# Graph attention on 8192 nodes: column groups for f, another order of loads and steps ahead of row 0, the mean in row 2, the last row on VectorE

## The chip, the cores and the metric

One core of a Trainium2 chip runs the kernel. The metric is device microseconds of one execution. TensorE is written PE (PEld is its weight load), VectorE DVE, ScalarE ACT, GpSimd POOL, SyncE SP; ACTq and SPq are the queues in which ACT and SP issue DMAs.

## The reference, cut to what matters

```python
h    = relu((x - mean(x)) / sqrt(var(x) + 1e-5))      # per row of x, 8192 x 256
g    = inlayer2 @ W.T + b                             # 8192 x 128
f1, f2 = g @ w1 + b1, g @ w2 + b2                     # one number per node each
L    = leaky_relu(f1[:, None] + f2[None, :], 0.01) - 1e9 * (adj == 0)
out  = x + softmax(L, axis=-1) @ h                    # adj is 8192 x 8192, int32
```

## The kernel before, in words

The output is made in 64 row tiles ("rows") of 128 nodes. For a row, the 128 x 8192 piece of adj (4 MB) comes in two halves (c = 0, 1) of four parts (g). ACT turns each part into a mask (L554), DVE makes unnormalised weights of it from the packed vectors `b_word` (per column) and `c_word` (per row) (`weights`, L824), DVE transposes them in eight strips of 1024 nodes (`turn`, L834) into one of four slots of `wT`, and PE multiplies each strip with the 16-bit parts of h in `H` (`products`, L1024 and L1026, 24 matmuls a strip), into `acc`. A 257th column gives the sum of weights. Then DVE makes its reciprocal (`finish_0` to `finish_2`, L843, L848, L853), ACT scales (`scale_rows`, L561), POOL adds x and, for a node with no neighbours, the mean of h (`finish`, L474, L476, L479), and SP stores. Each engine follows its own written list; semaphores order them.

Ahead of row 0 stands a start. inlayer2 (strips 0 to 7) and x (strips 0 to 7) are loaded in strips of 1024 nodes, 1 MB each, half issued by SP (quadrants 0, 1) and half by ACT (quadrants 2, 3). Since f1 and f2 are linear in inlayer2, `U` = W.T with w1 and w2 is made first; DVE transposes each strip of inlayer2 in two instructions (`turn_in2`, L718; there are two slots, so strip k waits for f of strip k - 2) and PE multiplies it with `V` (`f_of_strip`, L979): eight fp32 matmuls, one for each block of 32 features. `V` is made of the values of U spread over 128 columns, so that the results of the four quadrants of nodes stand apart. Strips 0 to 3 make chunk 0 of f, strips 4 to 7 chunk 1. ACT copies a chunk out of PSUM (`f_to_sbuf`, L532), DVE transposes it and takes the maximum (`chunk_f`, L751 to L756), PE and DVE bring the global maximum F to all partitions (L1003, L785, L1005), and from F come `D_big` and `D_inv` on ACT (L615, L616), the exponentials of b (`b_exponents` on PE, L987, then `b_of_chunk` on ACT, L537) and of c (L796, L1011, L622). DVE packs b and c (L809, L810), and `weights(0, 0, 0)` is the first of row 0 (L824 at 58.64 us).

The statistics of x are made beside that: strips 0 and 1 on ACT (`sums`, `squares`, L584), the others on DVE (`raw_stats`, L765, and `variance`, L773), the power of -1/2 on POOL (`rstds`, L411). Values of h are made by ACT and POOL and split into two 16-bit parts by ACT, POOL and DVE (`low_of_values`, L804). Rows 0 and 1 are interleaved by hand. The mean of h is summed by PE in between (`sum_of_values`, L1038), scaled by DVE (`h_sum`, L918), spread by PE (`hm_ps`, L1071) and copied by DVE (`h_mean`, L954); POOL's `finish` of row 0 waits for it, and SP, whose list has the store of row 0 ahead of the load of row 4's adj, waits for that `finish`.

Of the kernel before, what the change touches and what calls it, by code (L numbers as in the profile page):

```python
# [27 lines left out]
ALU = mybir.AluOpType  # L28
# [7 lines left out]
P = 128  # L36
B = 32
# [8 lines left out]
def graph_attention(nc, x, adj, inlayer2, W, b, w1, b1, w2, b2, out):  # L46
# [26 lines left out]
    with ExitStack() as ctx:  # L73
# [65 lines left out]
        F_ps = small[:, 1, 384:385]  # L139
        hs_ps = small[:, 1, 0:D]  # L140
# [37 lines left out]
        def h_slot(n):  # L178
# [4 lines left out]
        V = h_f32[:, 1, :, :].rearrange("p t d -> p (t d)").rearrange(  # L183
            "p (m i) -> p m i", m=FM)
# [25 lines left out]
        f_rows_ready = sem("f_rows_ready")  # L210
        f2_of_ready = sem("f2_of_ready")
# [46 lines left out]
        o_ready = sem("o_ready")  # L258
        o_stored = [sem(f"o_stored{i}") for i in range(2)]
# [103 lines left out]
        def _(sp):  # L363
# [4 lines left out]
            load_x(sp, 1, 4, (0, 1))  # L368
# [17 lines left out]
            for i in range(2):  # L386
                sp.wait_ge(o_ready, ROWS - 1 + i)
                sp.dma_start(out_rows[ROWS - 2 + i], o_sb[:, i, :]).then_inc(o_stored[i], 16)
            for i in range(2):
                sp.wait_ge(o_stored[i], 16 * ROWS // 2)  # L390

        @block.gpsimd
        def _(pool):
# [6 lines left out]
            rstd_order = (0, 2, 1, 3, 4, 5, 6, 7)  # L400
# [69 lines left out]
            def finish(I, par, half):  # L470
                pool.wait_ge(o_stored[par], 16 * half)
# [52 lines left out]
        def _(act):  # L524
# [94 lines left out]
            b_of_chunk(1)  # L619
            values(0)  # L620
# [67 lines left out]
            for i in range(2):  # L688
                scale_rows(ROWS - 2 + i, i, ROWS // 2 - 1)

        @block.vector
        def _(dve):
# [83 lines left out]
            for k in range(2, NS):  # L776
                turn_in2(k)
# [326 lines left out]
```

## Time and profile before

| | |
|---|---|
| runs of before | 1448.3, 1448.55, 1449.22 us; median 1448.55 |
| profiled execution | 1447.21 us; its span 1445.4 us |
| PE busy | 1408.1 us (97%) |
| DVE busy | 1279.7 us (89%) |
| granted clock, mean | 0.989 of 2.4 GHz |

The span runs from the first to the last instruction or landing of the program; 1.81 us of the profiled time lie around it. Busy shares are averages: the start, the passage into row 2 and the end have limits of their own. An engine's `xN` counts records; each fp32 matmul makes two.

### The profile page before, as it was taken

How to read it: one execution, taken by the hardware profiler on the slowest of the kernel's cores; microseconds unless marked ns; L12 is line 12 of the kernel's file. 1: busy time of each engine (PE TensorE's matmuls, PEld its weight loads, DVE VectorE, ACT ScalarE, POOL GpSimd, SP SyncE). 2: the span in 40 equal slices, each digit the busy share in tenths (PEclk: the TensorE clock that was granted, in tenths of full speed). 3: DMA queues.
4: the chain of work that ended last, by engine and by line, in shares of the span. 5: the costliest groups of instructions: out<-in, count | busy, mean ns of one | idle time of the engine just before them, and what ended most of it. 6: DMA issues, size and time to landing. Idle time of an engine off the chain costs nothing.

```text
span 1445.4 us, 33386 instructions
## 1 busy us (share of the span) xinstructions
PE 1408.1 (97%) x12623; PEld 1246.3 (86%) x12623; DVE 1279.7 (89%) x1313; ACT 612.4 (42%) x714; POOL 267.6 (19%) x269
## 2 busy tenths in 40 slices
PE   8489999999999999999999999999999999999998
PEld 7377888888888888888888888888888888888887
DVE  5899999989899898989989898998989989898994
ACT  2895344344444343444434344343434434344430
POOL 0582111101111110111111011111101111110111
PEclk9789999999999999999999999999999999999999
DMA  9978999999999999999999999999999999999940
GB/s 301 310 181 181 234 230 230 231 232 220 208 211 215 209 211 209 215 209 210 215 209 210 207 216 211 209 215 209 210 207 217 209 211 215 207 212 207 215 103 8
DMA packets 110168, 302.43 MB, mean 209 GB/s; under 512 B 11716, under 2 KB 44612, under 8 KB 110148
## 3 DMA queue, kind: packets, MB, share of 16 engines
q1 hardware_dynamic: 100144, 289.58, 89.4%
q10 hardware_dynamic: 10004, 12.59, 2.9%
q8 instruction: 12, 0.20, 0.1%
q14 instruction: 8, 0.07, 0.0%
HBM read 293.73 MB, written 8.39 MB: 209 GB/s over the span
## 4 chain that ended last, share of the span: by engine, by line
PE 94%; ACT 2%; DVE 2%; DMA 1%; issue 1%; ACTq 0%; POOL 0%; SPq 0%; POOLq 0%; DVEq 0%
PE acc L1024 61%; PE acc L1026 30%; PE rp L979 2%; DMA adj_sb<-in_adj_dram 1%; DVE wgt L824 1%; ACT h_f L570 1%; DVE wT L834 0%; ACT H L576 0%; PE rp L993 0%; ACT o_room L584 0%; DMA w<-in_L_gnn_w_dram 0%; PE small L966 0%; ACT rp L554 0%; DVE b_word L810 0%; ACT mask L554 0%
## 5 line engine op out<-in xcount | busy, mean ns | idle before, releaser
L1024 PE MATMUL acc<-H,wT 128*128 128x257 f16 x8192 | 1356.2, 273 | 9.7 <-DVE wT L834 6.9
L1026 PE MATMUL acc<-H,wT 128*128 128x257 f16 x4096 | 1120.0, 273 | 0.0
L1024 PEld LDWEIGHTS acc<-H,wT 128*128 128x128 bf16 x8192 | 802.1, 98 | 113.0 <-DVE wT L834 6.9
L554 ACT ACTIVATE mask<-adj_sb 128x1024 bf16<-128x1024 int32 x504 | 519.2, 1053 | 542.8 <-DVE wgt L824 428.8
L834 DVE STREAM_TRANSPOSE wT<-wgt 128x1024 f32<-128x1024 f32 x512 | 634.0, 1239 | 129.2 <-PE acc L1026 129.1
L824 DVE SCALAR_TENSOR_TENSOR wgt<-b_word,c_word,mask 128x1024 f32<-128x1024 f32 x504 | 626.9, 1256 | 0.0
L1026 PEld LDWEIGHTS acc<-H,wT 128*128 128x128 f16 x4096 | 401.5, 98 | 50.5
L474 POOL TENSOR_TENSOR x_res<-o_room,x_res 128x256 f32<-128x256 f32 x64 | 66.5, 1039 | 1115.2 <-ACT o_room L561 1069.5
L561 ACT ACTIVATE o_room<-acc,r_den 128x256 f32<-128x256 f32 x64 | 30.2, 471 | 251.0 <-DVE r_den L853 251.0
L479 POOL TENSOR_TENSOR o_room<-o_room,x_res 128x256 f32<-128x256 f32 x64 | 82.3, 1287 | 5.3
L476 POOL TENSOR_SCALAR o_room<-h_mean,no_nb 128x256 f32<-128x256 f32 x64 | 60.8, 950 | 0.0
L979 PE MATMUL rp<-wT,h_f 128*128 128x256 f32 x128 | 28.0, 381 | 0.0
L979 PEld LDWEIGHTS rp<-wT,h_f 128*128 128x128 f32 x128 | 24.5, 192 | 3.3
L570 ACT ACTIVATE h_f<-H,h_add,h_mul 128x256 f32<-128x256 f32 x48 | 24.7, 588 | 1.0 <-issue 1.0
L467 POOL TENSOR_TENSOR H<-h_f,H 128x1024 f16<-128x1024 f32 x8 | 17.8, 2226 | 4.0 <-ACT H L576 4.0
L411 POOL TENSOR_TENSOR rstd<-var_eps,minus_half 128x8 f32<-128x8 f32 x8 | 14.7, 1845 | 13.8 <-DVE var_eps L773 13.7
L1045 PE MATMUL small<-ones 128*128 128x128 f32 x20 | 4.6, 429 | 11.8 <-DVE wgt L824 11.8
L765 DVE BATCH_NORM_STATS2 stats<-H 128x6 f32<-128x512 f32 x24 | 15.3, 688 | 0.8 <-DMA H<-in_x_dram 0.8
L843 DVE TENSOR_SCALAR no_nb<-acc 128x1 f32<-128x1 f32 x64 | 7.7, 120 | 9.2 <-PE acc L1026 9.2
L1045 PEld LDWEIGHTS small<-ones 128*128 128x128 f32 x20 | 4.3, 331 | 12.0 <-DVE wgt L824 12.0
L718 DVE STREAM_TRANSPOSE wT<-wgt 128x1024 f32<-128x1024 f32 x8 | 9.5, 1222 | 5.7 <-DMA wgt<-in_L_gnn_inlayer_dram 3.6
L718 DVE STREAM_TRANSPOSE wT<-adj_sb 128x1024 f32<-128x1024 f32 x8 | 9.5, 1225 | 4.3 <-PE rp L979 4.3
(91 smaller groups left out, 173.2 us busy)
## 6 DMA issues: line engine op xcount, KB each, us to landing
adj_sb<-in_adj_dram SPq DMA_DIRECT2D x504, 512.0 KB, 8.6
x_res<-in_x_dram SPq DMA_DIRECT2D x64, 128.0 KB, 4.0
out_dram<-o_room SPq DMA_DIRECT2D x64, 128.0 KB, 4.2
H<-in_x_dram ACTq DMA_DIRECT2D x16, 256.0 KB, 12.2
H<-in_x_dram SPq DMA_DIRECT2D x16, 256.0 KB, 12.7
adj_sb<-in_adj_dram ACTq DMA_DIRECT2D x8, 512.0 KB, 13.1
wgt<-in_L_gnn_inlayer_dram ACTq DMA_DIRECT2D x8, 256.0 KB, 9.0
wgt<-in_L_gnn_inlayer_dram SPq DMA_DIRECT2D x8, 256.0 KB, 9.6
```

The source lines that it names most:

```text
L474: nc.gpsimd.tensor_tensor(x_res[:, par, :], o_raw[:, par, :], x_res[:, par, :], ALU.add).then_inc(pool_step, 1)
L476: nc.gpsimd.tensor_scalar(o_sb[:, par, :], h_mean[:, :], no_nb[:, par:par + 1], None, ALU.mult).then_inc(pool_step, 1)
L479: nc.gpsimd.tensor_tensor(o_sb[:, par, :], o_sb[:, par, :], x_res[:, par, :], ALU.add).then_inc(o_ready, 1)
L554: nc.scalar.activation(place, adj_sb[:, c, g * CQ:(g + 1) * CQ], ACT.Relu, scale=M_SCALE).then_inc(m_ready, 1)
L561: nc.scalar.activation(o_raw[:, par, :], acc[:, par, 0:D], ACT.Copy, scale=r_den[:, par:par + 1]).then_inc(scaled, 1)
L570: nc.scalar.activation(h_slot(n)[:, t, :], x_stage(n // 2)[:, j % TS, :], ACT.Relu, scale=h_mul[:, j:j + 1], bias=h_add[:, j:j + 1]).then_ ...
L718: nc.vector.transpose(in2T[:, k % 2, :, :].rearrange("p m (t s) -> p t m s", t=TS)[:, HALF * e:HALF * (e + 1), :, :], in2_stage(k)[:, HALF ...
L824: nc.vector.scalar_tensor_tensor(out=wgt[:, wgt_slot(I, c), g, :], in0=b_word[:, c * CQ:(c + 1) * CQ], scalar=c_word[:, bass.ds(Q * I + g, ...
L834: nc.vector.transpose(wT[:, wT_slot(I, k), :, :].rearrange("p t (g r) -> p g t r", g=Q), wgt[:, wgt_slot(I, c), :, s * SQ:(s + 1) * SQ]).t ...
L979: mm = pe.matmul(rp[:, k // SC, SQ * (k % SC):SQ * (k % SC + 1)], V[:, m, :], in2T[:, k % 2, m, :], start=(m == 0), stop=(m == FM - 1))
L1024: pe.matmul(acc[:, par, 0:DV], w_hi[:, slot, t, :], H[:, j, part, 0:DV], start=(j == 0 and part == 0), stop=False)
L1026: mm = pe.matmul(acc[:, par, 0:DV], w_lo[:, slot, t, :], H[:, j, 0, 0:DV], start=False, stop=(j == ROWS - 1))
```

## The change

1. Start, f: `V` has 32 columns instead of 128. Each strip's eight matmuls are 128 x 32 x 256, the four blocks of an inner loop going to four groups of 32 output partitions, in two rounds. The four groups hold partial sums; after DVE's transpose of a chunk, PE adds them with four small matmuls (`f_sums`), and DVE takes the sum from there. Behind each strip PE gets four fp32 matmuls of ones into a scratch place (`keep_busy(4)`).
2. Start, order: x strip 1 is loaded ahead of inlayer2 strips 6 and 7; ACT's part of strip 7 of inlayer2 is issued behind `sums(0)`. On DVE the transpose and maximum of chunk 0 stand ahead of strip 7, the statistics of x strips 2 and 3 in other places. On ACT `squares(1)` stands ahead of `f_to_sbuf(1)`, and ACT's two issues for x strip 7 stand behind `b_of_chunk(1)`. On POOL `rstds(1)` comes earlier and `rstds(3)` later.
3. Row 2: `h_sum`, its matmul and `h_mean` leave the passage between rows 1 and 2. DVE makes `h_sum` in strip step 0 of row 2, PE spreads it behind strip 1, DVE copies `h_mean` in step 5 instead of 2.
4. End: the last row is finished by two instructions on DVE, and its store is issued in two halves, by SP and by ACT.

```diff
-            load_in2(eng, 4, 8, quadrants)
+            load_in2(eng, 4, 6, quadrants)
+            load_x(eng, 1, 2, quadrants)
...
+            load_in2(sp, 6, 8, (0, 1))
-            load_x(sp, 1, 4, (0, 1))
+            load_x(sp, 2, 4, (0, 1))
...
-                for m in range(FM):
-                    mm = pe.matmul(rp[:, k // SC, SQ * (k % SC):SQ * (k % SC + 1)], V[:, m, :], in2T[:, k % 2, m, :],
-                                   start=(m == 0), stop=(m == FM - 1))
+                for e in range(2):
+                    for g in range(Q):
+                        m = 2 * g + e
+                        mm = pe.matmul(rp[B * g:B * (g + 1), k // SC, SQ * (k % SC):SQ * (k % SC + 1)], V[:, m, :],
+                                       in2T[:, k % 2, m, :], start=(e == 0), stop=(e == 1))
                 mm.then_inc(f_done, 1)
+            def f_sums(c):
+
+                pe.wait_ge(f_cols_ready, c + 1)
+                pe.wait_ge(pick_ready, Q + 1)
+                parts = f_cols[:, c * CQ:(c + 1) * CQ].rearrange("p (j a o v) -> p a j o v", a=Q, o=2, v=Q)
+                for a in range(Q):
+                    mm = pe.matmul(f_sum_ps[B * a:B * (a + 1), c * ROWS:(c + 1) * ROWS], same[:, :],
+                                   parts[:, a, :, :, 0], start=True, stop=True)
+                mm.then_inc(f_sum_ps_ready, 1)
...
+            def keep_busy(n):
+                for _ in range(n):
+                    pe.matmul(acc[:, 0, 0:P], ones[:, :], ones[:, :], start=True, stop=True)
...
-            dve.wait_ge(h_sum_done, 1)
-            nc.vector.tensor_scalar(h_sum[:, :], hs_ps, 1.0 / (H_SCALE * N), None, ALU.mult).then_inc(h_sum_ready, 1)
             weights(2, 2, 0)
...
-                    if is_row(I, 2) and u == 2:
+                    if is_row(I, 2) and u == 0:
+                        dve.wait_ge(h_sum_done, 1)
+                        nc.vector.tensor_scalar(h_sum[:, :], hs_ps, 1.0 / (H_SCALE * N), None,
+                                                ALU.mult).then_inc(h_sum_ready, 1)
+                    if is_row(I, 2) and u == 5:
...
+            nc.vector.scalar_tensor_tensor(out=x_res[:, 1, :], in0=acc[:, 1, 0:D], scalar=r_den[:, 1:2],
+                                           in1=x_res[:, 1, :], op0=ALU.mult, op1=ALU.add).then_inc(last_sum, 1)
+            dve.wait_ge(last_sum, 1)
+            nc.vector.scalar_tensor_tensor(out=o_sb[:, 1, :], in0=h_mean[:, :], scalar=no_nb[:, 1:2],
+                                           in1=x_res[:, 1, :], op0=ALU.mult, op1=ALU.add).then_inc(last_ready, 1)
```

PE, from the last warm-up ahead of f to the one ahead of row 0, in the kernel before (`rp<-wT,h_f` is f of a strip, `rp<-mask` the exponents of b, `tiny` the maximum):

```order
L993 MATMUL rp<-ones 128x128 x9
L979 MATMUL rp<-wT,h_f 128x256 x64
L987 MATMUL rp<-mask 128x512 x2
L1003 MATMUL small<-ident,tiny 1x128
L1005 MATMUL small<-tiny,ones 128x1
L987 MATMUL rp<-mask 128x512 x2
L1011 MATMUL small<-low,mask 128x64 x4
L1045 MATMUL small<-ones 128x128 x10
```

PE in the changed kernel, from strip 5 on (`acc<-ones` is the filler, `small<-wgt,same` is `f_sums`):

```order
L1020 MATMUL rp<-wT,h_f 32x256 x8
L1012 MATMUL acc<-ones 128x128 x4
L1020 MATMUL rp<-wT,h_f 32x256 x8
L1012 MATMUL acc<-ones 128x128 x4
L1030 MATMUL small<-wgt,same 32x64 x4
L1020 MATMUL rp<-wT,h_f 32x256 x8
L1012 MATMUL acc<-ones 128x128 x4
L1038 MATMUL rp<-mask 128x512 x2
L1030 MATMUL small<-wgt,same 32x64 x4
L1069 MATMUL small<-ident,tiny 1x128
L1071 MATMUL small<-tiny,ones 128x1
L1038 MATMUL rp<-mask 128x512 x2
```

Between the last transposed strip and F stand now the fillers, two sums over the groups, and the first exponents of b ahead of the second sum.

DVE in the kernel before, from the transposes of inlayer2 strips 4 to 7 on (two instructions a strip; `BN_STATS` is `raw_stats`):

```order
L718 STREAM_TRANSPOSE wT<-adj_sb 128x4x8x32 x8
L751 STREAM_TRANSPOSE wgt<-mask 128x1024
L752 COPY f_col<-wgt 128x64
L754 TENSOR_REDUCE tiny<-f_col 128x1
L765 BN_STATS stats<-H 128x6 x2
L751 STREAM_TRANSPOSE wgt<-mask 128x1024
L752 COPY f_col<-wgt 128x64
L754 TENSOR_REDUCE tiny<-f_col 128x1
L756 TENSOR_TENSOR tiny<-tiny 128x1
L765 BN_STATS stats<-H 128x6 x2
L783 TENSOR_TENSOR tiny<-cst 128x1
L785 TENSOR_REDUCE tiny<-small 1x1
```

DVE in the changed kernel, from the same strips on:

```order
L731 STREAM_TRANSPOSE wT<-adj_sb 128x4x8x32 x6
L764 STREAM_TRANSPOSE wgt<-mask 128x1024
L770 COPY f_col<-small 128x64
L772 TENSOR_REDUCE tiny<-f_col 128x1
L731 STREAM_TRANSPOSE wT<-adj_sb 128x4x8x32 x2
L783 BN_STATS stats<-H 128x6 x4
L764 STREAM_TRANSPOSE wgt<-mask 128x1024
L770 COPY f_col<-small 128x64
L772 TENSOR_REDUCE tiny<-f_col 128x1
L774 TENSOR_TENSOR tiny<-tiny 128x1
L791 TENSOR_SCALAR var_eps<-stats 128x8
L808 TENSOR_TENSOR tiny<-cst 128x1
```

Strip 7 now stands behind the transpose of chunk 0 and behind a copy that needs PE's sum over the groups, and the second chunk behind all statistics of x strip 2.

DVE at the passage into row 2, from the reciprocal of row 0 on, in the kernel before:

```order
L853 RECIPROCAL r_den<-den 128x1
L918 TENSOR_SCALAR h_sum<-small 128x256
L824 SCALAR_TENSOR_TENSOR wgt<-b_word,c_word,mask 128x1024 x2
L834 STREAM_TRANSPOSE wT<-wgt 128x4x8x32
L824 SCALAR_TENSOR_TENSOR wgt<-b_word,c_word,mask 128x1024 x2
L834 STREAM_TRANSPOSE wT<-wgt 128x4x8x32
L824 SCALAR_TENSOR_TENSOR wgt<-b_word,c_word,mask 128x1024
L834 STREAM_TRANSPOSE wT<-wgt 128x4x8x32
L954 COPY h_mean<-small 128x256
```

and in the changed kernel:

```order
L875 RECIPROCAL r_den<-den 128x1
L846 SCALAR_TENSOR_TENSOR wgt<-b_word,c_word,mask 128x1024 x2
L856 STREAM_TRANSPOSE wT<-wgt 128x4x8x32
L846 SCALAR_TENSOR_TENSOR wgt<-b_word,c_word,mask 128x1024
L976 TENSOR_SCALAR h_sum<-small 128x256
L846 SCALAR_TENSOR_TENSOR wgt<-b_word,c_word,mask 128x1024
L856 STREAM_TRANSPOSE wT<-wgt 128x4x8x32
L846 SCALAR_TENSOR_TENSOR wgt<-b_word,c_word,mask 128x1024
L856 STREAM_TRANSPOSE wT<-wgt 128x4x8x32
```

`h_sum` has gone behind the first weights that follow row 2's first transpose, and the copy of `h_mean` out of this stretch.

## Rows read from the trace of the kernel before

**Rows 1.** The page, part 1 (busy time) and part 2 (granted clock in 40 slices)
```profile
PE 1408.1 (97%) x12623; PEld 1246.3 (86%) x12623; DVE 1279.7 (89%) x1313; ACT 612.4 (42%) x714; POOL 267.6 (19%) x269
...
PEclk9789999999999999999999999999999999999999
```

**Rows 2.** Windows: busy time (records) of each engine, granted clock, DMA share, GB/s
```profile
58.73:110.06 51.33, 38.58 (x357) 31.53 (x357) 51.23 (x52) 49.22 (x73) 43.74 (x57) 0.79 0.84 206
...
132.58:1439.55 1306.97, 1306.97 (x11880) 1162.29 (x11880) 1168.62 (x1171) 524.31 (x546) 206.19 (x189) 1.00 0.93 206
```

**Rows 3.** Waits of PE, 0 to 150 us: total us, times, longest
```profile
PE acc L1024 <- DVE wT L834: 6.9, 5, 4.3
```

**Rows 4.** Timeline, start: start us, length us, engine, line, instruction [idle before]
```profile
14.52 28.01 PE L979 MATMUL rp<-wT,h_f 128*128 128x256 f32 x128
...
35.73 2.37 DVE L718 STREAM_TRANSPOSE wT<-adj_sb 128x1024 f32<-128x1024 f32 x2 [1.08 <-PE rp L979]
...
37.34 0.42 ACT L584 ACTIVATE o_room<-H 128x256 f32<-128x256 f32 x1 [3.41 <-DMA H<-in_x_dram]
...
38.03 1.20 DVE L751 STREAM_TRANSPOSE wgt<-mask 128x1024 f32<-128x1024 f32 x1
```

**Rows 5.** The last two inlayer2 issues of each queue: durations, starts, time to landing
```profile
L333 ACTq DMA_DIRECT2D adj_sb<-in_L_gnn_inlayer_dram x2: 1397/1964/2532, 18.6 to 21.2; - x2
...
DMA to landing us min/median/max: 11.9/12.8/13.2
```

**Rows 6.** Timeline of ACT and its queue behind the last strip of f
```profile
42.57 1.01 ACT L532 COPY mask<-rp 128x1024 f32<-128x1024 f32 x1 [1.68 <-PE rp L979]
...
46.46 2.85 ACTq L333 DMA_DIRECT2D H<-in_x_dram  x1
...
49.34 1.42 ACTq L333 DMA_DIRECT2D H<-in_x_dram  x1
...
50.80 0.26 ACT L615 ACTIVATE D_big<-f_rel 128x64 f32<-128x64 f32 x1 [3.27 <-issue]
```

**Rows 7.** Windows (columns as in rows 2), then timeline: VectorE up to the first weights
```profile
35.73:58.64 22.91, 12.18 (x51) 8.42 (x49) 18.21 (x35) 16.32 (x47) 8.80 (x10) 0.87 1.08 333
...
58.64 1.27 DVE L824 SCALAR_TENSOR_TENSOR wgt<-b_word,c_word,rp 128x1024 f32<-128x1024 f32 x1
```

**Rows 8.** Timeline of PE: ten warm-up matmuls; then windows of PE alone
```profile
63.57 4.64 PE L1045 MATMUL small<-ones 128*128 128x128 f32 x20 [11.83 <-DVE wgt L824]
...
86.60:90.05 3.45, 0.00 (x0) 1.00 0.95 255
90.05:93.50 3.45, 2.86 (x14) 0.51 1.02 274
```

**Rows 9.** Timeline, passage from row 1 to row 2, PE and VectorE
```profile
124.91 0.42 DVE L918 TENSOR_SCALAR h_sum<-small 128x256 f32<-128x256 f32 x1 [2.30 <-PE small L1038]
...
127.44 0.60 PE L1071 MATMUL small<-h_sum,ones 128*128 128x256 f32 x2
129.15 0.38 PE L1024 MATMUL acc<-H,wT 128*128 128x257 f16 x2 [1.11 <-DVE wT L834]
...
132.58 0.39 PE L1024 MATMUL acc<-H,wT 128*128 128x257 f16 x2 [0.63 <-DVE wT L834]
```

**Rows 10.** Timeline, the mean vector, SyncE's load of row 4, its mask
```profile
134.76 0.39 DVE L954 COPY h_mean<-small 128x256 f32<-128x256 f32 x1
...
139.90 5.07 SPq L338 DMA_DIRECT2D adj_sb<-in_adj_dram  x8
...
152.94 2.00 ACT L554 ACTIVATE mask<-adj_sb 128x1024 bf16<-128x1024 int32 x2 [9.58 <-DMA adj_sb<-in_adj_dram]
```

**Rows 11.** Timeline, the end, VectorE, ScalarE, SyncE's queue
```profile
1439.97 0.16 DVE L853 RECIPROCAL r_den<-den 128x1 f32<-128x1 f32 x1
1440.17 0.47 ACT L561 ACTIVATE o_room<-acc,r_den 128x256 f32<-128x256 f32 x1 [17.00 <-DVE r_den L853]
...
1443.23 0.34 SPq L388 DMA_DIRECT2D out_dram<-o_room  x1
```

More of the change, by code:

```diff
@@ L139, in graph_attention @@
         F_ps = small[:, 1, 384:385]
+        f_sum_ps = small[:, 0, 256:256 + 2 * ROWS]
         hs_ps = small[:, 1, 0:D]
@@ L258, in graph_attention @@
         o_ready = sem("o_ready")
+        last_sum = sem("last_sum")
+        last_ready = sem("last_ready")
+        last_stored = sem("last_stored")
         o_stored = [sem(f"o_stored{i}") for i in range(2)]
@@ L687, in _ @@
             row_tiles(act, body, ahead=1)
-            for i in range(2):
-                scale_rows(ROWS - 2 + i, i, ROWS // 2 - 1)
+            scale_rows(ROWS - 2, 0, ROWS // 2 - 1)
+            act.wait_ge(last_ready, 1)
+            act.dma_start(out_rows[ROWS - 1][P // 2:P], o_sb[P // 2:P, 1, :]).then_inc(last_stored, 16)
         @block.vector
@@ L774, in variance @@
                                         ALU.add).then_inc(var_ready, 1)
-            for k in range(2, NS):
-                turn_in2(k)
-            chunk_f(0)
+            turn_in2(2)
+            turn_in2(3)
+            turn_in2(4)
+            turn_in2(5)
+            turn_in2(6)
+            chunk_turn(0)
+            chunk_max(0)
+            turn_in2(7)
             raw_stats(16, 20)
-            chunk_f(1)
             raw_stats(20, 24)
+            chunk_turn(1)
+            chunk_max(1)
+            variance(2)
             dve.wait_ge(u_ready, Q + 1)
@@ L856, in _ @@
             then_wait(pack_b(0))
+            raw_stats(28, 32)
             then_wait(pack_b(1))
+            variance(3)
             dve.wait_ge(c_exp, 1)
@@ L994, in _ @@
             pe.wait_ge(u_ready, Q)
-            for k in range(NS):
-                f_of_strip(k)
+            f_of_strip(0)
+            keep_busy(4)
+            f_of_strip(1)
+            keep_busy(4)
+            f_of_strip(2)
+            keep_busy(4)
+            f_of_strip(3)
+            keep_busy(4)
+            f_of_strip(4)
+            keep_busy(4)
+            f_of_strip(5)
+            keep_busy(4)
+            f_of_strip(6)
+            keep_busy(4)
+            f_sums(0)
+            f_of_strip(7)
+            keep_busy(4)
             pe.wait_ge(f2_of_ready, 1)
             b_exponents(0)
+            f_sums(1)
             pe.wait_ge(ident_ready, 1)
@@ L1069, in _ @@
             products(1, 1, 7)
-            pe.wait_ge(h_sum_ready, 1)
-            pe.matmul(hm_ps, ones[:, :], h_sum[:, :], start=True, stop=True).then_inc(h_mean_ps_ready, 1)
             pe.wait_ge(scaled, 1)
@@ L1080, in body @@
                     products(I, par, k)
+                    if is_row(I, 2) and k == 1:
+                        pe.wait_ge(h_sum_ready, 1)
+                        pe.matmul(hm_ps, ones[:, :], h_sum[:, :], start=True,
+                                  stop=True).then_inc(h_mean_ps_ready, 1)
             row_tiles(pe, body, ahead=1)
```

64 lines of the change are left out of this document (37 added, 27 removed).

## The prediction

> **What bounds the kernel now.** I read the page first. PE is busy for 97% of the span and its clock is at the full level in nearly all slices [rows 1]: almost all of the time is matmuls that this change leaves alone. So the next question is where PE last waited, and the windows answer it: from 132.58 to 1439.55 us PE has no idle time [rows 2]. That stretch holds 495 strips, 2.640 us each. Nothing that happens on another engine there costs anything, as long as it stays inside its cover. The time can change in three places only: in what ends at 132.58, in the 5.85 us behind 1439.55, and by a new stall in between.
>
> Then I ask what sets 132.58. The waits of PE show 6.9 us on DVE's transposes up to 150 us [rows 3], 4.3 of them in one piece. DVE is busy for 51.23 of 51.33 us between 58.73 and 110.06 [rows 2]. So in rows 0 and 1 DVE is the bound, and PE's stalls there are its echo. DVE gets through this list as early as it may begin it: its beginning is the first `weights`, at 58.64 [rows 7]. A microsecond at 58.64 is, to first order, one at the end. Ahead of 58.64, DVE is busy for only 18.21 of 22.91 us [rows 7]; the 4.70 idle us are what the start can still give. The last 110 to 133 us have a limit of their own, the passage into row 2.
>
> **Sum, term 1: the start (f).** Before, the 128 records of f take 28 us without a pause, 3.48 us a strip [rows 4], which is slower than a strip's two transposes (2.37): DVE waits 1.08 us each time for PE. In column groups, a strip's 16 records would take a quarter if the four run side by side, 0.87 us; no row here shows such groups, so my bounds are that quarter and all of the 3.48. That removes the PE bound, but not what is below it: the last issues of inlayer2 start at 21.2 us and need up to 13.2 to land [rows 5], so the last strip is there at 34.3, and before it was transposed at 35.73. No more than 1.4 us could be had there. And now x strip 1 takes that place in the queues: strip 6 lands at 34.3, strip 7 where x strip 1 landed. ACT waited for x strip 1 until 37.34 [rows 4], so strip 7 is there 3 us later than now. The work on DVE from strip 6 on is then the 18.21 us of before and one more strip: 34.3 + 2.37 + 18.21 = 54.9 us, and to that come the waits. This is the place where the order of the change matters. Strip 7 is put behind `chunk_max(0)`, which needs PE: f of strip 6, four fillers, `f_sums(0)`.
>
> With PE at full clock: strip 6 transposed at 36.7; f 0.87, fillers 8 records of 128 columns, 0.87 (half of a 256-column record's 0.217 each), sums about 0.5 with latency: 39.0 to 39.2. DVE has the transpose of chunk 0 (1.20 [rows 4]) meanwhile, until 37.9; it waits 1.3. For chunk 1 PE has f, fillers and the first exponents of b (about 3.6 together) against DVE's statistics and transpose (3.8): a wait of about 0.6. The two steps to F cost 0.7, small gaps 0.5 as before (4.70 less the three long waits). First `weights`: 54.9 + 1.3 + 0.6 + 0.7 + 0.5 = 58.0, or 0.6 us earlier than now. ACT's move of x strip 7 belongs to this term: in the trace the two issues block the ScalarE list for 2.85 and 1.42 us and D_big stands at 50.80 [rows 6]; without them b is ready up to 2 us earlier, but DVE, full by then with moved statistics, uses little of that.
>
> **The clock decides the term.** PE now has 1.7 us of work a strip, fillers included. An issue takes some 1.4 us in the full queue [rows 5], two a strip in each queue, so strips come every 2.8 us. Strip 5 is two places ahead of strip 6, with x strip 1 between: landed by 28.7, transposed by 31.1, done on PE at 32.8. Then PE has nothing until 36.7, about 4 us. What PE did before its clock fell in this trace: no record from 86.60 to 90.05, and then a window at 0.51 although PE was 83% busy in it [rows 8]. The gap ahead of strip 6 is about as long as the wait around that one, 4.3 us [rows 3]. At the low level ten fp32 matmuls of 128 columns take 4.64 us, 0.213 us a record once running [rows 8], twice as long. Then f of strip 6 takes 1.74, fillers 1.71 and sums 0.6: 41.0 instead of 39.1, 1.8 us lost. The fillers, meant as cover, lie on the path here. If the clock is back by the end of this burst (4 us without a pause; between 90.05 and 93.50 it came back after such a one), chunk 1 runs at full rate: first `weights` at 59.8, **1.2 us later than now**. I take this value. If it is low in chunk 1 too, f, fillers and exponents take 7 us against DVE's 3.8: another 3.5 to 4 us, first `weights` at about 63.7, 5 us later.
>
> The Trainium skill, page "TensorE: Matmul & The Clock Gate", Part 1 (HAM oscillation), says that short bursts of matmuls with waits for DMA between them start cold each time; the window at 0.51 agrees with it. The same page, Part 3, gives 2.38 times for three column tiles side by side; by that figure f would take 1.46 us a strip, an estimate, and the first `weights` would stand about a microsecond later. No row of this trace can bear that figure out.
>
> **Term 2: into row 2.** DVE waits 2.30 us for PE's sum and needs 0.42 for `h_sum` [rows 9]; without them the weights and the first transpose of row 2 come 2.65 us earlier, at 126.3. PE is then free at 127.44, instead of starting strip 0 at 129.15 [rows 9]. Strip 0 ends at 130.08. Strip 1's transpose ended at 132.55 and ends at 132.55 - 2.65 + 0.42 = 130.3 (0.42 for `h_sum`, now in its path): 0.2 stall. Strip 1 ends at 132.94, the matmul for the mean takes 0.43, strip 2 starts at 133.4; before it was 132.58 + 2.64 = 135.22. Gain 1.8 us.
>
> What is late next: `h_mean`. It moves from 134.76 to behind strip 5, in my count 139.8. POOL's `finish` waits for it, SP's store waits for POOL, and behind the store in SP's list are row 4's loads, issued at 139.90 [rows 10], when the reads had nothing else to do. They go out at about 145.0, and the first masks move from 152.94 to 158.0, done at 159.0. DVE wants them at about 156.3 (from 139.8 on: the copy, eight weights, eight transposes at 1168.62 / 990 = 1.18 each plus gaps). It waits 2.7 us, does two weights and a transpose until 162.7; PE wants that strip at 133.4 + 11 x 2.64 = 162.4. So 0.3 us come back. Net 1.5.
>
> **Term 3: the end.** The reciprocal ends at 1440.13, the store is issued at 1443.23 [rows 11]; between them an ACT and three POOL instructions. Two DVE instructions of 128x256 take their place. The kernel before has none of that kind; `h_sum`, one input from PSUM, took 0.42 [rows 9], a 1024-column weights 1.27 (a quarter is 0.32) [rows 7], ACT's scaling 0.47 [rows 11]. I take 0.42 each: store issued at 1441.1. The two halves land about as the whole did, 2.2 us later. Gain 2.15, bounds 1.9 to 2.4.
>
> **Sum.** -1.2 + 1.5 + 2.15 = 2.45 us less. Against the profiled execution's own 1447.21 this is 1444.8; the median of the runs stands 1.34 above it, so 1448.55 - 2.45 = **1446.1**.
>
> **Rivals.**
> - *The clock stays up (or is back within strip 6).* For: fillers behind each strip, and strips 4 and 5 follow closely. Against: the gap of 4 us. First `weights` 58.0: 0.6 + 1.5 + 2.15 = 4.25, 1444.3.
> - *The start gets clearly shorter.* f ends early, DVE finds its data, the 4.70 us of idle shrink to 2: 1442.5. Against: strip 7 lands 3 us later than before.
> - *Low clock through chunk 1.* For: DVE-paced bursts of 1.7 us. -5 + 1.5 + 2.15: slower by 1.4, 1449.9, too little to be told from no change.
> - *Column groups don't run side by side, at low clock.* Each strip then needs 6.9 us: strip 6's f, fillers and sums end at 46, DVE waits 8 us instead of 1.3, and strip 7's f (3.5 at full rate) adds 2.6. First `weights` at 67.4: -8.8 + 1.5 + 2.15, slower by 5.1, 1453.7. The side changes where the start loses more than 3.65 us, and is measurable beyond 6.5. For: in the trace every fp32 record takes its full time, whatever it feeds. Against: the four groups use different columns of the array.
> - *Row 4's loads too late.* Each further microsecond on POOL or in the loads is one of PE stall in row 3, at strip 5; 1 to 2 us, 1447.5. POOL's first `finish` has such spread.
>
> **How the numbers follow.** I give 0.40 to the forecast (own range 1445.0 to 1447.5, a quarter of it beyond the bound of "faster"), 0.27 to the clock staying up, 0.06 to the shorter start, 0.14 to the low clock through chunk 1, 0.07 to groups in series, 0.06 to row 4. About 0.2% (2.9 us) is what a measurement of this kernel can tell from no change: faster means below 1445.65. Faster: 0.27 + 0.06 + 0.10 = 0.43. Slower: 0.07 and a part of the low clock's spread, 0.11. The rest, 0.46, is the same. The range is 1443.3 to 1450.0: it leaves out the shortest start and the series.
>
> **What the profile after would show.** Term 1: the granted clock between 30 and 50 us; f of a strip in 0.9 us (1.7 if low) or in 3.5; DVE waiting for PE between the two chunks; the first `weights` at 59.8. Term 2: row 2 starting with no wait over 0.3 us, no stall of PE at about 162. Term 3: two instructions of 0.4 us and a span that ends 3.7 us behind the last matmul instead of 5.85. I am wrong if the first `weights` move and the end doesn't follow, which would mean that DVE's list from 58.73 to 110.06 has slack, in its waits for POOL inside instructions for example.

## The result, and the profile after

Over 16 runs the changed kernel takes 1452.68 us (1448.59 to 1454.83), the kernel before 1448.70 us (1447.25 to 1449.38) on the same chips. The ratio is 1.0025, with a 95% interval of 1.0018 to 1.0032: slower by 0.25%, about 4 us. The profiled execution of after took 1454.47 us (span 1452.7), 7.3 us more than the profiled one of before.

Part 1 and part 2 of the page of after, the rows that answer to [rows 1], and then the longest waits of PE in its first 190 us (total, times, longest):

```profile
PE 1405.4 (97%) x12703; PEld 1236.8 (85%) x12703; DVE 1281.2 (88%) x1315; ACT 611.2 (42%) x713; POOL 265.7 (18%) x266
...
PEclk9789999999999999999999999999999999999999
...
PE rp L1020 <- DVE wT L731: 11.2, 5, 5.0
PE acc L1090 <- DVE wT L856: 4.9, 2, 4.5
PE acc L1090 <- ACT o_room L572: 3.6, 1, 3.6
```

Against [rows 1] PE is busy 2.7 us less, in a span 7.3 us longer. In the waits there are two new ones, on the transposes of inlayer2 (L731) in the start and on `o_room`, which ScalarE writes (L572). The old wait on `wT`, 6.9 us in [rows 3], is now 4.9 us in two pieces.

**Start.** Timeline of PE in after, from f of strip 4 on (start, length, engine, line, instruction, idle before and what ended it):

```profile
28.95 1.94 PE L1020 MATMUL rp<-wT,h_f 128*32 128x256 f32 x16 [5.00 <-DVE wT L731]
30.82 2.08 PE L1012 MATMUL acc<-ones 128*128 128x128 f32 x8
...
38.04 1.94 PE L1020 MATMUL rp<-wT,h_f 128*32 128x256 f32 x16 [2.33 <-DVE wT L731]
39.91 1.76 PE L1012 MATMUL acc<-ones 128*128 128x128 f32 x8
41.60 0.41 PE L1030 MATMUL small<-wgt,same 128*32 128x64 f32 x8
44.98 1.94 PE L1020 MATMUL rp<-wT,h_f 128*32 128x256 f32 x16 [2.97 <-DVE wT L731]
46.84 1.70 PE L1012 MATMUL acc<-ones 128*128 128x128 f32 x8
```

A strip of f takes 1.07 us at full clock and 1.94 at half; before it took 3.48 [rows 4]. The clock was down for strip 4 already (5.00 us idle ahead of it), and for strips 6 and 7 and the fillers behind them. In between it came back: the granted clock was 0.50 from 38 to 41 us, 1.00 from 42 to 44 us, where PE waited for strip 7, and 0.50 again from 45 to 48 us. Its mean from 14.46 to 45.00 us was 0.83. VectorE in the same stretch and up to the first `weights`:

```profile
35.62 2.37 DVE L731 STREAM_TRANSPOSE wT<-adj_sb 128x1024 f32<-128x1024 f32 x2 [3.69 <-DMA adj_sb<-in_L_gnn_inlayer_dram]
...
42.07 0.22 DVE L770 COPY f_col<-small 128x64 f32<-128x64 f32 x1 [2.96 <-PE small L1030]
...
42.55 2.37 DVE L731 STREAM_TRANSPOSE wT<-adj_sb 128x1024 f32<-128x1024 f32 x2
...
62.42 1.26 DVE L846 SCALAR_TENSOR_TENSOR wgt<-b_word,c_word,rp 128x1024 f32<-128x1024 f32 x1
```

Strip 6 is transposed at 35.62, with 3.69 us of idle time ahead of it for its load, and strip 7 only at 42.55, because `chunk_max(0)` (L770) stands ahead of it and waits 2.96 us for PE. The first `weights` stand at 62.42 instead of 58.64 [rows 7]: 3.8 us later.

**Row 2 and row 3.** Timeline of VectorE, PE, POOL, SyncE's queue and ScalarE around the mean vector and the masks of row 4, and a window (busy time and records of each engine, granted clock, DMA share, GB/s):

```profile
136.37 0.60 PE L1147 MATMUL small<-h_sum,ones 128*128 128x256 f32 x2
...
143.06 0.38 DVE L980 COPY h_mean<-small 128x256 f32<-128x256 f32 x1
...
143.52 1.70 POOL L485 TENSOR_TENSOR x_res<-o_room,x_res 128x256 f32<-128x256 f32 x1 [25.82 <-DVE h_mean L980]
...
147.57 0.36 SPq L389 DMA_DIRECT2D out_dram<-o_room  x1
...
148.82 4.68 SPq L343 DMA_DIRECT2D adj_sb<-in_adj_dram  x8
...
161.50 3.90 ACT L565 ACTIVATE mask<-adj_sb 128x1024 bf16<-128x1024 int32 x4 [14.33 <-DMA adj_sb<-in_adj_dram]
171.18 3.90 ACT L565 ACTIVATE mask<-adj_sb 128x1024 bf16<-128x1024 int32 x4 [5.78 <-DMA adj_sb<-in_adj_dram]
174.98 0.45 ACT L572 ACTIVATE o_room<-acc,r_den 128x256 f32<-128x256 f32 x1
...
166.46 0.40 PE L1090 MATMUL acc<-H,wT 128*128 128x257 f16 x2 [0.46 <-DVE wT L856]
...
175.56 0.61 PE L1090 MATMUL acc<-H,wT 128*128 128x257 f16 x2 [3.65 <-ACT o_room L572]
...
170.00:182.00 12.00, 8.35 (x52) 6.14 (x50) 10.95 (x9) 4.98 (x6) 3.32 (x3) 0.72 1.03 224
```

The passage itself went as forecast: PE has no wait there, and the matmul of the mean takes 0.60 us. But the copy of `h_mean` is at 143.06 instead of 134.76, and row 4's loads at 148.82 instead of 139.90 [rows 10]. The second half of the masks starts at 171.18, and ScalarE's scaling stands behind it, at 174.98; in the kernel before it was at 165.62, behind masks that began at 161.81:

```profile
161.81 3.90 ACT L554 ACTIVATE mask<-adj_sb 128x1024 bf16<-128x1024 int32 x4 [4.97 <-DMA adj_sb<-in_adj_dram]
165.62 0.46 ACT L561 ACTIVATE o_room<-acc,r_den 128x256 f32<-128x256 f32 x1
```

PE has to have that scaling ahead of strip 7 of row 3, and idles for 3.65 us. From 170 to 182 us its granted clock is 0.72: this wait is followed by a stretch at half clock, in which a pair of matmuls takes up to 0.64 us instead of 0.38, until 181.2 us.

**End.** The last instructions of VectorE and the two halves of the last store:

```profile
1448.90 0.48 DVE L989 SCALAR_TENSOR_TENSOR x_res<-acc,r_den,x_res 128x256 f32<-128x256 f32 x1
1449.41 0.48 DVE L992 SCALAR_TENSOR_TENSOR o_room<-h_mean,no_nb,x_res 128x256 f32<-128x256 f32 x1
...
1449.93 0.55 SPq L396 DMA_DIRECT2D out_dram<-o_room  x1
...
1449.93 0.57 ACTq L702 DMA_DIRECT2D out_dram<-o_room  x1
```

They answer to [rows 11]: the stores are issued 1.07 us behind the end of the reciprocal (1448.86) instead of 3.10, but the span ends 2.77 us behind the issue instead of 2.2.

The start's 3.8 us are 3.5 by the last transposes of row 1 (112.29 against 108.75). So the profiled executions differ by 3.5 (start) - 1.9 (passage) - 1.4 (end) and what is left for row 3, 7.1, together 7.3 us. The 7.1 is a remainder; the first experiment checks it.

### The profile page after: what moved, and what is told of

The parts are those of the page before. It is cut to its first block, busy times and chain, and to the rows that moved or that the text cites. A ratio compares the mean times of both kernels' runs of the same rounds, so it can differ in the third digit from the quotient of the medians.

```text
span 1452.7 us, 33546 instructions
## 1 busy us (share of the span) xinstructions
PE 1405.4 (97%) x12703; PEld 1236.8 (85%) x12703; DVE 1281.2 (88%) x1315; ACT 611.2 (42%) x713; POOL 265.7 (18%) x266
## 4 chain that ended last, share of the span: by engine, by line
PE 88%; ACT 3%; DMA 3%; SPq 2%; DVE 2%; issue 1%; POOL 0%; ACTq 0%; DVEq 0%; POOLq 0%
PE acc L1090 58%; PE acc L1092 29%; DMA adj_sb<-in_adj_dram 2%; ACT mask L565 1%; SPq L338 1%; ACT h_f L581 1%; DMA adj_sb<-in_L_gnn_inlayer_dram 1%; ACT H L587 0%; ACT rp L565 0%; SPq L343 0%; PE rp L1020 0%; DVE stats L783 0%; DVE wgt L846 0%; PE acc L1012 0%; DVE b_word L832 0%
## 5 line engine op out<-in xcount | busy, mean ns | idle before, releaser
L856 DVE STREAM_TRANSPOSE wT<-wgt 128x1024 f32<-128x1024 f32 x512 | 633.7, 1239 | 131.2 <-PE acc L1092 131.1
L572 ACT ACTIVATE o_room<-acc,r_den 128x256 f32<-128x256 f32 x63 | 29.8, 473 | 228.8 <-DVE r_den L875 228.8
L1020 PE MATMUL rp<-wT,h_f 128*32 128x256 f32 x128 | 11.9, 506 | 11.2 <-DVE wT L731 11.2
L731 DVE STREAM_TRANSPOSE wT<-adj_sb 128x1024 f32<-128x1024 f32 x8 | 9.5, 1224 | 9.2 <-DMA adj_sb<-in_L_gnn_inlayer_dram 9.1
L1020 PEld LDWEIGHTS rp<-wT,h_f 128*32 128x32 f32 x128 | 4.1, 134 | 15.2 <-DVE wT L731 12.2
L1012 PEld LDWEIGHTS acc<-ones 128*128 128x128 f32 x64 | 9.7, 233 | 4.8 <-issue 4.8
```

The source lines that it names most:

```text
L572: nc.scalar.activation(o_raw[:, par, :], acc[:, par, 0:D], ACT.Copy, scale=r_den[:, par:par + 1]).then_inc(scaled, 1)
L856: nc.vector.transpose(wT[:, wT_slot(I, k), :, :].rearrange("p t (g r) -> p g t r", g=Q), wgt[:, wgt_slot(I, c), :, s * SQ:(s + 1) * SQ]).t ...
L1020: mm = pe.matmul(rp[B * g:B * (g + 1), k // SC, SQ * (k % SC):SQ * (k % SC + 1)], V[:, m, :], in2T[:, k % 2, m, :], start=(e == 0), stop=( ...
```

## Experiments

All times are medians in us, beside the kernel before on the same chip (1448.57 to 1448.96). Each kernel was run 10 or 11 times, the ninth, twelfth and fifteenth 5 times. The theory: in row 2 nothing is wrong but the place of `h_mean`, whose delay reaches PE a row later; and the start is late by itself. The rivals stand in each expectation.

**1. The copy of h_mean behind strip 3.** The kernel after with

```diff
-                    if is_row(I, 2) and u == 5:
+                    if is_row(I, 2) and u == 3:
```

Expected: 

> The kernel after, with the copy of h_mean on VectorE two places earlier (behind strip 3 of row 2 instead of strip 5). Theory A: the loss comes in row 3, where PE waited 3.65 us at strip 7 for ScalarE's scaling (behind late masks) and its clock then fell for 7 us. With the copy 4 to 5 us earlier, that stall and the fall of the clock are gone: 3.8 us less (what is left of the medians' difference of 4.0 after +3.5 for the start, -1.9 for the passage, -1.4 for the end) to 7.1 us less (what the profiled execution shows): 1445.6 to 1448.9, likeliest 1447. Theory B: the loss is the late start, and the wait at strip 7 is the luck of one execution: 1452 to 1453, as after.

Measured: 1447.15 (1445.1 to 1449.29, 11 runs), ratio to before 0.9985 [0.9976, 0.9994]. One digit takes 5.5 us off and turns slower into faster. Its window over the same 12 us, and the issue and the scaling that moved:

```profile
143.01 5.68 SPq L343 DMA_DIRECT2D adj_sb<-in_adj_dram  x8
...
165.83 3.90 ACT L565 ACTIVATE mask<-adj_sb 128x1024 bf16<-128x1024 int32 x4 [6.56 <-DMA adj_sb<-in_adj_dram]
169.64 0.45 ACT L572 ACTIVATE o_room<-acc,r_den 128x256 f32<-128x256 f32 x1
...
170.00:182.00 12.00, 12.00 (x112) 10.68 (x110) 11.74 (x14) 3.99 (x5) 3.48 (x3) 1.00 1.03 229
```

PE runs 112 records in these 12 us, 0.107 us each; after had 52, so 60 x 0.107 = 6.4 us were lost there, 3.65 of them idle and some 2.8 by the clock (an upper bound, since some records can be missing).

**2 and 3. The row 2 part alone, on the kernel before**, once with `h_mean` behind strip 5 and once behind strip 3:

```diff
-            dve.wait_ge(h_sum_done, 1)
-            nc.vector.tensor_scalar(h_sum[:, :], hs_ps, ...)
...
+                    if is_row(I, 2) and u == 0:
+                        dve.wait_ge(h_sum_done, 1)
...
-                    if is_row(I, 2) and u == 2:
+                    if is_row(I, 2) and u == 5:    # 3 in the other
```

Expected with 5: 

> The kernel before with the row 2 part of the change alone (h_sum and its matmul inside row 2, h_mean behind strip 5). Theory A: 1.9 us earlier into row 2, h_mean 4.7 us later, so that the loads of row 4 go out 4.7 us later; ScalarE's scaling then ends 3.2 us behind the time at which PE wants it at strip 7 of row 3, and the fall of the clock costs up to 3.4 more: 1450.0 to 1453.4. Theory B (the loss is in the start; this part is worth what was predicted): 1.5 us faster than before, 1447.2.

Expected with 3: 

> As the second kernel, but h_mean copied behind strip 3. Theory A: the passage's 1.9 us come, and the loads of row 4 go out at about 140, as before; no stall at strip 7 of row 3: 1446.8. Theory B: the same as with strip 5, within 0.5 us. A third theory, that the matmul of the mean inside row 2 is itself the cost, gives 1449 or more here too.

Measured: 1452.70 (ratio 1.0023 [1.0014, 1.0032]) and 1446.94 (0.9986 [0.9977, 0.9995]). In the first PE waits for ScalarE at the same place:

```profile
173.12 0.45 ACT L561 ACTIVATE o_room<-acc,r_den 128x256 f32<-128x256 f32 x1
...
173.71 0.61 PE L1026 MATMUL acc<-H,wT 128*128 128x257 f16 x2 [4.48 <-ACT o_room L561]
```

A loss as large as that of the whole change appears with this part alone, and the same part with the copy two strips earlier is worth 2.0 us, what the prediction had for the passage (1.8).

**4. The end alone, on the kernel before** (the diff's parts on `finish`, the last two stores and the two VectorE instructions). Expected: 

> The kernel before with the end part alone: the last row finished by two VectorE instructions, its store in two halves. From the profile after, 4.4 us behind the last matmul instead of 5.85: 1.4 us less, 1447.3. The prediction had 2.15 less, 1446.5. A rival, that the two stores end no sooner than one: 1448.7.

Measured: 1447.31, 1.65 us less (0.9988 [0.9979, 0.9997]).

**5. SyncE's list reordered, h_mean still behind strip 5.** In SyncE's list the store of row 0 and the load of row 2's x (`x_res`) go from ahead of row 4's loads to between their two halves; for that the list of one more pair of rows is written out (`ahead=2`). The kernel after with

```diff
+                    if is_row(I, 3) and n == Q - 1:
+                        sp.wait_ge(o_ready, 1)
+                        sp.dma_start(out_rows[0], o_sb[:, 0, :])...
+                        sp.dma_start(x_res[:, 0, :], x_rows[2])...
-                    if n == NS - 1 and not (is_row(I, 0) or is_row(I, 1)):
+                    if n == NS - 1 and not (is_row(I, 0) or is_row(I, 1) or is_row(I, 2)):
...
-            row_tiles(sp, body, ahead=1)
+            row_tiles(sp, body, ahead=2)
```

Expected: 

> The kernel after with h_mean left behind strip 5, but in SP's list row 0's store and the residual load of row 2 stand behind the first mask loads of row 4 instead of ahead of them. Theory A (what makes the late h_mean costly is the order of SP's list: its store waits for h_mean by way of POOL, and row 4's loads stand behind it): the loads go out at about 140 to 143 us, no stall at strip 7 of row 3, and the time is that of the run with the earlier copy, 1447.2, within 0.7. Theory B (the late copy costs by another way, on VectorE or POOL): as after, 1452 to 1453.

Measured: 1447.12 (0.9989 [0.9980, 0.9998]), as the first experiment. SyncE's queue in it:

```profile
134.50 1.74 SPq L343 DMA_DIRECT2D adj_sb<-in_adj_dram  x4
...
147.82 0.36 SPq L389 DMA_DIRECT2D out_dram<-o_room  x1
...
148.70 1.88 SPq L343 DMA_DIRECT2D adj_sb<-in_adj_dram  x4
```

The copy is as late as in after (143.31), and so is row 0's store at 147.82. But the four loads of the first half are out at 134.50, ahead of it (I had expected 140). They land from 146.1 to 152.9, and the other four, issued at 148.70, from 156.3 to 163.5; the last one of after lands at 171.09. PE does not wait. What costs is the order of SyncE's list, by way of ScalarE's, and not the late copy as such.

**6, 7 and 9. The fillers of the start**, all with the copy behind strip 3. Sixth: 22 matmuls behind strip 3, 12 behind strip 5, 9 ahead of strip 7, the others as they were. Seventh: no fillers. Ninth: none on the path from strip 6 on, and long ones in the waits behind strips 3, 5 and 6; those behind strips 0, 1, 2 and 4 stay:

```diff
             f_of_strip(3)
-            keep_busy(4)
+            keep_busy(22)
...
             f_of_strip(5)
-            keep_busy(4)
+            keep_busy(20)
             f_of_strip(6)
-            keep_busy(4)
             f_sums(0)
+            keep_busy(12)
             f_of_strip(7)
-            keep_busy(4)
```

Expected of the sixth: 

> As the first experiment (copy behind strip 3), and the fillers of TensorE made long enough to cover its waits for the strips of inlayer2: 22 matmuls instead of 4 behind strip 3, 12 behind strip 5, 9 ahead of strip 7. Theory C (the start is late because the clock is down when strips 6 and 7 come): the clock stays up from 15 to 55 us, f of strips 6 and 7 and the fillers behind them take 2 us each time instead of 3.7, the first weights stand at 59 to 60 instead of 62.4, and the time falls by 2 to 3 us to 1444.2 to 1445.2. Theory D (the landing of strip 7 and the work on VectorE behind it set the start, whatever the clock): within 0.7 of 1447.15.

Expected of the seventh: 

> As the first experiment, with all the 4-matmul fillers between the strips of f taken out. Theory C2 (in this execution the fillers did not hold the clock, and stood on the path behind strips 6 and 7 with 1.7 us each): the clock falls earlier, but f_sums(0) and the exponents of b come up to 1.7 us earlier each; first weights 1.5 to 3 us earlier, 1444.5 to 1446. The rival, that the fillers were worth their time: at the lower clock the chain behind them costs more than they did, 1448 or more.

Expected of the ninth: 

> As the first experiment (copy behind strip 3), but fillers only where TensorE has nothing else to do: 22 matmuls behind strip 3, 20 behind strip 5, none behind strip 6, 12 behind f_sums(0), none behind strip 7. In the run with 22, 12 and 9 (first weights 60.27, median 1445.3) the clock had fallen again for f of strip 6, and it and its fillers took 3.8 us ahead of f_sums(0). If clock and fillers on the path are what is left, VectorE gets f_sums(0) and f_sums(1) 2.2 to 2.5 us earlier, of which ScalarE's values of b let it use two thirds: first weights 58.3 to 58.9, time 1443.4 to 1444. If the landing of strip 7 sets the start, it stays at 1445.0 to 1445.6.

Measured: 1445.30, 1445.43 and 1442.72, against 1447.15. The seventh fell into its range; the sixth just missed its range (1444.2 to 1445.2), and the ninth gave 0.7 us more than its own (1443.4 to 1444). No fillers at all is better than the fillers of the change, although the clock is then at 0.50 from 30 to 40 us. In the sixth f of strip 6 still took 1.94 us, behind 2.08 us of idle time:

```profile
37.20 1.94 PE L1020 MATMUL rp<-wT,h_f 128*32 128x256 f32 x16 [2.08 <-DVE wT L731]
39.06 1.89 PE L1012 MATMUL acc<-ones 128*128 128x128 f32 x8
```

In the ninth the idle time ahead of it is 0.33 us, f takes 1.07, and `f_sums(0)` follows at once:

```profile
37.59 1.07 PE L1020 MATMUL rp<-wT,h_f 128*32 128x256 f32 x16 [0.33 <-DVE wT L731]
38.72 0.41 PE L1030 MATMUL small<-wgt,same 128*32 128x64 f32 x8
39.05 2.94 PE L1012 MATMUL acc<-ones 128*128 128x128 f32 x24
```

The first `weights` stood at 60.27, 60.82 and 57.90, the last 0.4 us ahead of what I had given it.

**8 and 12. The kernel before with row 2 (behind strip 3) and the end, without and with the x issue moved:**

```diff
-            load_x(act, 7, 8, (2, 3))
             act.wait_ge(f2_rel_ready, 1)
...
             b_of_chunk(1)
+            load_x(act, 7, 8, (2, 3))
```

Expected without: 

> The kernel before with the row 2 part (h_mean behind strip 3) and the end part, and its own start. If the two add: 1448.96 - 2.02 - 1.65 = 1445.3. The difference to the first experiment is then what the start part costs: 1.9 us by the medians, against 3.5 to 3.8 by the first weights of one profiled execution. If they do not add (a stall moved to the next row): 1446.5 or more.

Expected with: 

> The kernel before with row 2 (h_mean behind strip 3), the end part and the last x issue moved behind the values of b on ScalarE, its start otherwise its own. The run without the move took 1445.17. If the issue delays D_big and with it b on the path (VectorE waited 1.6 to 2.7 us for b ahead of the first weights in the runs with before's start), the move gives 1 to 2 us: 1443.2 to 1444.2. If x strip 7 lands too late for its first reader, or VectorE was not waiting for ScalarE's list, no change: 1445.2.

Measured: 1445.17, as expected, and 1442.49 (0.9959 [0.9945, 0.9972]), 0.7 us below the range that I had given. The move alone is worth 2.7 us. ScalarE's exponential of f (`D_big`), in the eighth and then in the twelfth, shows why:

```profile
46.21 4.40 ACTq L336 DMA_DIRECT2D H<-in_x_dram  x1
50.64 1.50 ACTq L336 DMA_DIRECT2D H<-in_x_dram  x1
52.18 0.26 ACT L622 ACTIVATE D_big<-f_rel 128x64 f32<-128x64 f32 x1 [5.07 <-issue]
```

```profile
48.48 0.26 ACT L621 ACTIVATE D_big<-f_rel 128x64 f32<-128x64 f32 x1 [1.23 <-DVE f_rel L798]
```

**10 and 11. The loads in their old order.** Tenth: inlayer2 strips 4 to 7 ahead of x strip 1 again. Eleventh: besides, strip 7 transposed straight behind strip 6, `f_sums(0)` behind the first exponents, no fillers behind strips 6 and 7, and 22 instead of 4 behind strip 3.

Expected of the tenth: 

> As the first experiment, with the first loads in the order of before: inlayer2 strips 4 to 7, then x strip 1 and on, column groups, fillers and VectorE's order as in the kernel after. If the change of the load order is what makes the start late (VectorE sat idle 3.7 us ahead of strip 6, waiting for its load), strip 6 lands some 2.3 us earlier, and the first weights come that much earlier than 62.5: median 1444.9 to 1445.2. If x strip 1 is then missed just as much by ScalarE and by VectorE's statistics, no gain: 1446.8 to 1447.5.

Expected of the eleventh: 

> As the run with the loads in the order of before, and besides strip 7 transposed straight behind strip 6 instead of behind chunk_max(0), f of strips 6 and 7 back to back without fillers, f_sums(0) behind the first exponents of b, and 22 fillers behind strip 3. It has column groups, but not the other edits of the start. Strips 6 and 7 land at 32.5 and 34.3, transposed by 37.2 (35.73 + 2.37 = 38.1 in the kernel before): the limit by loads that the prediction gave, 0.9 us ahead of before, at most 1.4. First weights 58 to 59, 3.5 to 4.5 us earlier than the first experiment's 62.5: 1442.7 to 1443.7. If the extra step through PE (f_sums) costs as much as the groups save: 1445.2, as with before's own start.

Measured: 1446.43 and 1446.69; both missed, by 1.2 and 3 us, and both lie outside the rivals' values too. In the eleventh strips 6 and 7 were transposed by 37.9, close to the 37.2 that I had given them. Timeline of ScalarE and VectorE in the eleventh:

```profile
46.62 0.99 ACT L541 COPY mask<-rp 128x1024 f32<-128x1024 f32 x1
...
44.02 0.23 DVE L767 COPY f_col<-small 128x64 f32<-128x64 f32 x1 [5.01 <-PE small L1027]
```

Now x strip 1 is the late one. ScalarE's list has its sums and squares ahead of the copy of f's second half out of PSUM (L541), and this one comes at 46.62 (46.65 in the tenth), 6.7 us behind the matmuls that it copies; and VectorE waits 5.01 us for `f_sums(0)`, which stands on PE behind the exponents of b at the half clock (3.78 us).

**13. The x issue moved, alone, on the kernel before.** Expected: 

> The kernel before with the last x issue moved, and nothing else. With the row 2 and end parts beside it the move gave 2.7 us (1445.17 to 1442.49). If the parts add: 1448.85 - 2.7 = 1446.1. If the move only pays once row 2 is mended: 1447.5 or more. The prediction had counted it at next to nothing.

Measured: 1446.25 (0.9983 [0.9974, 0.9992]), 2.3 us less.

**14. The first experiment with the x issue back in its old place.** Expected: 

> As the first experiment (the kernel after, copy behind strip 3), with the last x issue back in its old place, ahead of the wait for F in ScalarE's list. If the move pays in the changed start too, this is 2.7 us slower than 1447.15: 1449.9, and the column groups, fillers and load order together then cost 4.7 us by themselves. If in the changed start the move pays nothing, because ScalarE is idle there before F comes (D_big at 53 instead of 51): 1447.2, and what the change of the start gives away is that the move is no longer worth its 2.7.

Measured: 1447.39 (0.9991 [0.9982, 1.0000]); the rival was right, no difference to 1447.15. The same instruction there:

```profile
46.91 4.90 ACTq L338 DMA_DIRECT2D H<-in_x_dram  x6
53.11 0.26 ACT L627 ACTIVATE D_big<-f_rel 128x64 f32<-128x64 f32 x1 [5.19 <-DVE f_rel L813]
```

**15. The eleventh, mended.** ScalarE's list is that of the kernel before but for the last x issue: the copies of f's rows stand ahead of the squares, and x strip 4 is issued ahead of the sums of strip 1. `f_sums(0)` stands straight behind f of strip 7, and 7 fillers between strips 6 and 7. The part on f's second half:

```diff
-            squares(1)
             f_to_sbuf(1)
             load_x(act, 5, 6, (2, 3))
+            squares(1)
...
             f_of_strip(6)
+            keep_busy(7)
             f_of_strip(7)
+            f_sums(0)
             pe.wait_ge(f2_of_ready, 1)
             b_exponents(0)
-            f_sums(0)
```

Expected: 

> As the run with column groups only, and besides ScalarE's list in its order of before (the copy of f's rows ahead of the squares), f_sums(0) straight behind f of strip 7, and 7 fillers between strips 6 and 7. In the run without these VectorE waited 5.0 us for f_sums(0) behind the exponents at the low clock, and PE 5.0 us for the transposed chunk 1, because ScalarE copied its f rows only at 46.6, behind 8 sums and 8 squares of x strip 1, although f was done at 40. If those two places were why the loads in their old order gave nothing: the copy at 41.8, the first weights at 56.5 to 57.5 instead of 62, time 1441.5 to 1442.6. If the landing of x strip 1 holds the list at another place instead: 1445 to 1446.7.

Measured: 1442.64 (0.9959 [0.9945, 0.9972]); the copy at 41.89, the first `weights` at 58.25 instead of 61.95. The bounds of 1442.6 and of 57.5 for the `weights` were just missed, the other theory is far off. Which of its edits did most was not tried apart.

Three starts thus end at the same 1442.5 to 1442.7, some 6 us below before; the simplest of them is the kernel before with the x issue, the row 2 part with the copy behind strip 3, and the end (the twelfth). In their profiled executions the first `weights` stand at 57.90 (ninth), 56.71 (twelfth) and 58.25 (fifteenth): 1.5 us apart, while the medians are 0.2 apart. The first `weights` of one execution thus forecast a median to a microsecond at best; why these three meet was not looked at.

## Why the prediction was wrong, step by step

- **"Everything stands on 132.58, in 5.85 us at the end, and in a new stall in between"** was right, and the third of these decided.
- **Term 2, passage** ("Gain 1.8 us"): right, 2.0 measured.
- **Term 2, "So 0.3 us come back. Net 1.5"**: this step failed. Its way up to the masks was right: with 3.5 us more for the late start, its 139.8, 145.0 and 158.0 become 143.3, 148.5 and 161.5, against 143.06, 148.82 and 161.50. I followed the first four mask parts to VectorE, found 0.3 us of stall at strip 5 (measured 0.46 at 166.46), and stopped. The eight loads land some 2.3 us apart, from 154.3 on, the last at 171.09; ScalarE's other four masks wait for it, and the scaling of the accumulator is behind them in ScalarE's list. PE wants that scaling at strip 7, 171.9. In the kernel before the scaling ended at 166.08, 3.4 us ahead of the need (strip 7 of row 3 began 14 strips of 2.64 us behind 132.58, at 169.5). With the start's 3.5 us left out, the change moved the end of the scaling by 5.8 us (175.43 against 169.6) and PE's need by 1.2 us forward (171.9 against 173.1): 5.8 + 1.2 - 3.4 = 3.6 us of wait, 3.65 measured. And the half clock followed this wait and nearly doubled its cost (up to 6.4 us in the window of the first experiment). Together 5.5 us by medians (1452.68 to 1447.15, and the same by the fifth experiment). My rival "row 4's loads too late" had the cause, but priced it on VectorE's way at 1 to 2 us, with a chance of 0.06.
- **Term 1, the start** (-1.2): measured -2.0 (1447.15 against 1445.17, the same kernel with the start of before). The sign and the way, half clock for strips 6 and 7 with the fillers on the path, were right. I took the clock to be back for chunk 1. It was back at 42 us, but PE then waited 2.97 us for strip 7, and f of strip 7 and its fillers ran at half clock again, until 48.4: part of the rival "low clock through chunk 1" (the exponents of b behind them ran at the full clock, 1.88 us). The row that I leaned on was also misread: in [rows 8] the clock came back inside the window from 90.05 to 93.50, in a burst that begins at 90.64, so behind less than the "4 us without a pause". The 3.8 us between the two profiled executions overstate it: four other kernels with the start of before had their first `weights` at 59.80 to 60.19, and the profiled one of before at 58.64. That is about as much as the 1.34 us by which that execution stood under the median of its three runs.
- **The move of x strip 7** was counted at next to nothing ("DVE ... uses little of that"). It is worth 2.3 to 2.7 us on the start of before (8, 12, 13), and nothing in the changed start (14). There `D_big` waits for VectorE's f_rel 5.19 us, and the issues lie beside that wait; on the old start the two issues hold ScalarE for 5.9 us (eighth experiment; 4.3 in [rows 6]). So column groups, load order and fillers together cost 2.2 us where both starts are without the move (1447.39 against 1445.17) and 4.7 where both have it (1447.15 against 1442.49): they took back all that the move was worth, and 2.0 us more.
- **Term 3, the end** (2.15): 1.65 by medians, 1.4 in the profiled execution. The mis-sized items are the two instructions, 0.48 us each instead of 0.42, and the landing, 2.77 us behind the issue instead of 2.2: each half lands 2.0 and 2.3 us behind its issue, the whole store of before in 1.7.
- **Rival "groups in series"**: refuted. A strip's 16 records take 1.00 us from its start to that of the fillers at full clock, against 3.48. By the Trainium skill, page "TensorE: Matmul & The Clock Gate", Part 3 (2.38 times for three column tiles), f would take 1.46 us, an estimate; with four groups the trace has 3.48 / 1.00 = 3.5 times. Of the rule in Part 1 of that page that bursts with waits for DMA between them start cold, the trace of after shows strip 4 at 1.94 us behind 5.00 us of idle time, but not each time: strips 2 and 3, behind waits of 0.57 and 0.36 us, ran at the full clock (1.07 us each). And the window at 0.51 in [rows 8] stood behind a wait for VectorE, not for DMA.

The medians add up: 2.0 (start) - 2.0 (passage) + 5.5 (late h_mean) - 1.65 (end) = 3.9; measured 4.0. Start and late h_mean are themselves differences of these runs, so what the sum tests is that passage and end add (the eighth). Open stays why after spreads over 6 us: the profiles show one execution each.

## What to carry to other kernels

Moving a copy later is a move for everything that waits for it in any list: follow it through every in-order list that it reaches (here POOL, SyncE, the transfers, ScalarE), and to the last piece of a batch of loads and not the first, until it comes back to the engine that bounds the time. A filler that holds the clock belongs into idle time; in front of a result that somebody waits for, it costs its full length, and twice that when it fails to hold the clock. When two edits of one stage touch different engines, measure each alone: the better one may be hidden by the other.

## What the runs showed of the hardware

- Four fp32 matmuls of 32 weight columns each, put in four column groups, run side by side: 16 records of 256 columns in 1.00 us at the full clock and 1.87 at half (28.95 to 30.82), against 3.48 for full-width ones.
- Eight mask loads of one row land about 2.3 us apart, so that a row's loads take some 18 of the 21 us that its matmuls take: a delay of the loads is made up only slowly.
- A wait of 3.65 us in an otherwise unbroken stretch of matmuls was followed by the half clock; together they cost up to 6.4 us. A wait of 0.46 us, 9 us earlier, was not. In the start, where PE had paused several times before, shorter waits were too: 2.08 us (sixth experiment) and 1.95 us (eleventh, f of strip 7 at 1.94 us).
- The same two DMA issues on ScalarE held its list for 4.40 and 1.50 us in one execution and for 2.85 and 1.42 in another [rows 6]; `D_big` stands 1.38 us later in the first, which is about the difference between its first `weights`, at 59.99, and those at 58.64.
